# Two gated layers with a routed mixture of experts: row sums by VectorE from PSUM, their moments earlier in VectorE's order, POOL's powers behind three scatters

## The reference, cut to what matters

```
x = x + tanh(g_xattn[0]) * attention(layernorm(x), ctx, ctx)
x = x + tanh(g_ffn[0])   * ternary_ffn(layernorm(x))            # top 102 of 1024 kept per row
x = x + tanh(g_xattn[1]) * ssm(ctx, ctx, layernorm(x))          # 16 heads of 8 channels, length 256
x = x + tanh(g_ffn[1])   * moe(layernorm(x))                    # 64 experts, 6 per row, and a shared one

# ssm, per head: y = causal convolution of k_i * v_j with the head's kernel, + D * k_i * v_j
#                out_j = sum_i y_ij * q_i
# moe: softmax of x @ gate_w.T, top 6 of 64, weights normalised over the 6,
#      sum over the 6 of weight * expert(x), plus shared(x); expert = down(silu(gate) * up)
```

## Time and profile before

| | |
|---|---|
| median of three runs | 725.75 us (724.75 to 727.04) |
| the profiled execution | 725.16 us, its span 723.3 us |
| granted TensorE clock, mean | 0.929 |
| PE busy | 612.6 us, 85% |
| VectorE busy | 473.6 us, 65% |
| POOL busy | 434.3 us, 60% |
| ScalarE busy | 285.7 us, 40% |

### The profile page before, as it was taken

One profiled execution on the slowest core, in us unless ns is written; L12 is line 12 of the kernel. 1 busy time (PEld: TensorE's weight loads), 2 busy tenths in 40 slices (PEclk: granted clock), 3 DMA queues, 4 the chain that ended last, 5 costly groups with the idle time before them and its releaser, 6 DMA issues.

```text
span 723.3 us, 12095 instructions
## 1 busy us (share of the span) xinstructions
PE 612.6 (85%) x3072; PEld 472.9 (65%) x3072; DVE 473.6 (65%) x1607; ACT 285.7 (40%) x641; POOL 434.3 (60%) x483
## 2 busy tenths in 40 slices
PE   4789994873999958999998669999999999999920
PEld 2455552442988827777777458888888888888720
DVE  6898997998688768878875623454445454544425
ACT  3156777863355423444445213233323223233200
POOL 2697996130244421877777733677777777786660
PEclk9799997887999988999999669999999999999975
DMA  7457655695599955666663679999999999996878
GB/s 231 159 176 273 207 203 193 204 318 223 185 339 322 347 174 164 224 214 215 230 233 126 225 225 308 241 257 250 247 249 262 255 255 255 263 274 107 237 118 296
DMA packets 89050, 167.83 MB, mean 232 GB/s; under 512 B 11296, under 2 KB 53728, under 8 KB 88992
## 3 DMA queue, kind: packets, MB, share of 16 engines
q1 hardware_dynamic: 68096, 139.36, 57.6%
q0 software_dynamic: 20608, 27.82, 20.0%
q10 hardware_dynamic: 288, 0.01, 0.0%
HBM read 93.33 MB, written 73.81 MB: 231 GB/s over the span
## 4 chain that ended last, share of the span: by engine, by line
PE 55%; DVE 15%; issue 11%; DMA 8%; POOL 6%; ACT 3%; SPq 1%; DVEq 1%; POOLq 0%; ACTq 0%
PE psum L1123 12%; PE psum L951 8%; PE psum L1136 7%; PE psum L1127 6%; PE psum L1030 4%; PE psum L1141 4%; PE psum L1107 4%; POOL xs_rows L773 3%; DVE hh L1735 3%; PE psum L942 2%; DVE Z L1579 2%; PE psum L1041 2%; DMA acc<-hh,toki 2%; POOL acc L815 2%; PE psum L987 1%
## 5 line engine op out<-in xcount | busy, mean ns | idle before, releaser
L815 POOL DMA_INDIRECT acc<-hh,toki x128 | 187.9, 1468 | 80.5 <-DVE hh L2092 41.9
L2092 DVE TENSOR_SCALAR hh<-psum,wtok 96x256 f32<-96x256 f32 (+3 forms) x128 | 55.8, 477 | 131.8 <-issue 120.8
L773 POOL DMA_INDIRECT xs_rows<-Z,slot x96 | 98.2, 1023 | 38.5 <-issue 26.7
L1123 PE MATMUL psum<-qT,Z 128*128 128x192 f32 (+3 forms) x480 | 97.7, 347 | 0.0
L1123 PEld LDWEIGHTS psum<-qT,Z 128*128 128x128 f32 x480 | 81.0, 193 | 2.3
L690 POOL TENSOR_TENSOR rstd<-mv,neghalf 128x1 f32<-128x1 f32 (+1 forms) x48 | 33.6, 709 | 65.8 <-DVE mv L1843 57.6
L1402 ACT ACTIVATE qT<-psum 128x384 f32<-128x384 f32 (+3 forms) x64 | 33.6, 524 | 96.6 <-PE psum L1107 95.7
L872 PE MATMUL psum<-wt,hTs 128*128 128x512 f32 x128 | 59.7, 609 | 0.6 <-ACT hTs L1219 0.6
L951 PE MATMUL psum<-wt,hh 128*128 128x256 f32 x256 | 58.1, 380 | 0.0
L1136 PE MATMUL psum<-Z,hh 128*96 128x256 f32 (+3 forms) x240 | 56.7, 379 | 0.0
L1127 PE MATMUL psum<-qT,Z 128*112 128x192 f32 (+3 forms) x240 | 52.6, 342 | 0.0
(11 more groups left out here) (352 smaller groups left out, 1266.2 us busy)
## 6 DMA issues: line engine op xcount, KB each, us to landing
Z<-in_wexp SPq DMA_DIRECT2D x62, 496.0 KB, 4.1
xs_rows<-fill SPq DMA_DIRECT2D x64, 272.0 KB, 3.2
kv_rows<-Z SPq DMA_DIRECT2D x12, 688.0 KB, 3.9
kvb<-kv_rows SPq DMA_DIRECT2D x8, 688.0 KB, 6.0
Z<-co_rows SPq DMA_DIRECT2D x8, 688.0 KB
Z<-kv_rows SPq DMA_DIRECT2D x8, 688.0 KB, 6.3
Z<-xs_rows SPq DMA_DIRECT2D x24, 204.0 KB, 4.1
Z<-xs_rows SPq DMA_DIRECT2D x16, 272.0 KB, 3.8
```

Of the source, the lines that this page charges most:

```text
L773: pool.indirect_dma_start(out=xs_rows[:, :], out_offset=bass.IndirectOffsetOnAxis(ap=slot[:, t, k:k + 1], axis=0), in_=H[:, t, :], in_offs ...
L815: pool.indirect_dma_start(out=acc[a][:, :], out_offset=bass.IndirectOffsetOnAxis(ap=toki[0:p, g, j:j + 1], axis=0), in_=y_sb[0:p, s, j, :] ...
L1123: m = pe.matmul(pA[par][:, g * CAP:g * CAP + 2 * p], w[:, s, k, g * P:(g + 1) * P], xT[:, par, k, 0:2 * p], start=(k == 0), stop=(k == 1))
L2092: m = dve.tensor_scalar(y_sb[0:p, s, j, :], pY[par][0:p, j * D:(j + 1) * D], wtok[0:p, g, j:j + 1], None, ALU.mult)
```

## The change

PE's product of the rows with the identity goes, and the turned quarters start the sum in PSUM. ScalarE's `keep_rows` goes. VectorE adds the PSUM sum to the rows in place (one instruction of 128x512), ahead of the statistics, in `x3_moments`, which now holds the statistics too and signals them once for a pair. In VectorE's order `x3_moments(u)` moves ahead of `times_q(a)` for pairs from 2 on (behind it for pairs 0 and 1), `mean_shift(u)` stands behind `times_q(a)`, and `shared_hidden(w,2)` and `four(a)` behind that. POOL's power stands behind three scatters of every pair.

```
 POOL       for u in range(NPAIR):
                 pool.wait_ge(slots_ready, u + 1)
-                near = 3 if u in (0, NPAIR - 2) else K - 1
-                for k in range(near):
+                for k in range(3):
                     scatter(2 * u, k)
                 if u + 1 < NPAIR:
                     pow_pair(u + 1)
-                for k in range(near, K):
+                for k in range(3, K):
                     scatter(2 * u, k)
 PE x3_turn
-                pe.wait_ge(x_in[n // 2], 32)
-                for q in range(2):
-                    pe.matmul(x3p[:, q * D:(q + 1) * D], ident[:, :], X[:, 2 * n + q, :],
-                              start=(q == 0), stop=False, skip_group_check=True)
...
                             m = pe.matmul(x3p[:, q * D + l * P:q * D + (l + 1) * P], r[:, s_, l], ident[:, :],
-                                          start=False, stop=(s_ == 3), is_transpose=True, skip_group_check=True)
+                                          start=(q == 0 and l == 0 and s_ == 0), stop=(s_ == 3), is_transpose=True, skip_group_check=True)
 ACT
-            def keep_rows(u):
-                act.wait_ge(o3T_done, u + 1)
-                act.activation(X[:, 2 * u:2 * u + 2, :], x3p[:, :].rearrange("p (t d) -> p t d", t=2), ACT.Copy).then_inc(x3_done, 1)
 DVE
-            def x3_stats(n):
+            def x3_moments(n):
+                dve.wait_ge(x_in[n // 2], 32)
+                dve.wait_ge(o3T_done, n + 1)
+                rows = X[:, 2 * n:2 * n + 2, :]
+                dve.tensor_tensor(rows, rows, x3p[:, :].rearrange("p (t d) -> p t d", t=2), ALU.add).then_inc(x3_done, 1)
                 dve.wait_ge(x3_done, n + 1)
                 for t in range(2 * n, 2 * n + 2):
-                    alone(dve, "dve")
-                    dve.bn_stats(stats[:, t, :], X[:, t, :]).then_inc(stats_done, 1)
-
-            def x3_moments(n):
-                dve.wait_ge(stats_done, 2 * n + 2)
+                    m = dve.bn_stats(stats[:, t, :], X[:, t, :])
+                m.then_inc(stats_done, 1)
+                dve.wait_ge(stats_done, n + 1)
                 alone(dve, "dve")
...
-                if u == 1:
+                if u < 0:
                     times_q(a)
-                    x3_stats(u)
-                    shared_hidden(w, 0)
+                    four(a)
+                    times_q(b)
+                    four(b)
+                elif u < 2:
+                    times_q(a)
                     x3_moments(u)
-                    shared_hidden(w, 1)
+                    if w >= 0:
+                        shared_hidden(w, 0)
+                        shared_hidden(w, 1)
                     mean_shift(u)
                     four(a)
                     times_q(b)
-                    shared_hidden(w, 2)
+                    if w >= 0:
+                        shared_hidden(w, 2)
                     four(b)
                 else:
...
+                    shared_hidden(w, 0)
+                    shared_hidden(w, 1)
+                    x3_moments(u)
                     if heads:
                         times_q(a)
+                    mean_shift(u)
+                    shared_hidden(w, 2)
+                    if heads:
                         four(a)
...
                         times_q(b)
                         four(b)
```

More of the change, by code:

```diff
@@ L766, in _ @@
             pool.wait_ge(filled, 16 * (E + 3))
-            def pow_pair(n):
-                pool.wait_ge(var5_ready, n + 1)
-                pool.tensor_tensor(rstd[:, 2 * n:2 * n + 2], mv[:, 2 * n:2 * n + 2, 1], neghalf[:, 0:2], ALU.pow).then_inc(rstd5_ready, 1)
             def scatter(t, k):
@@ L776, in scatter, with pow_pair @@
                     in_=H[:, t, :], in_offset=None).then_inc(scattered, 16)
+            def pow_pair(n):
+                pool.wait_ge(var5_ready, n + 1)
+                pool.tensor_tensor(rstd[:, 2 * n:2 * n + 2], mv[:, 2 * n:2 * n + 2, 1], neghalf[:, 0:2], ALU.pow).then_inc(rstd5_ready, 1)
             pow_pair(0)
@@ L1380, in _ @@
                     continue
-                keep_rows(u)
                 if u >= 1:
@@ L1390, in _ @@
                 shared_silu(u, 0)
-                if u == 0:
-                    keep_rows(1)
                 shared_silu(u, 1)
@@ L1978, in _ @@
                     times_q(b)
-                    shared_hidden(w, 2)
+                    if w >= 0:
+                        shared_hidden(w, 2)
                     four(b)
                 else:
-                    if w >= 0:
-                        shared_hidden(w, 0)
-                        shared_hidden(w, 1)
+                    shared_hidden(w, 0)
+                    shared_hidden(w, 1)
+                    x3_moments(u)
                     if heads:
                         times_q(a)
+                    mean_shift(u)
+                    shared_hidden(w, 2)
+                    if heads:
                         four(a)
[L1988 to L1996, removed]
                         times_q(b)
-                    if heads:
                         four(b)
```

## The result

The changed kernel takes 734.12 us (median of 4 runs, 732.59 to 737.28); the kernel before, on the same chip, 725.44. The ratio is 1.0122, 95% interval 1.0085 to 1.016: slower by 8.7 us, where 725.3 had been forecast and 722.8 to 728.0 given as the range. The profiled execution took 734.11 us, its span 732.0.

A forecast was written before the change was run, and what follows sets the result against it. POOL's scatter stream was taken as the bound. First scatter +0.65, pair 2 0.97 later, pairs 2 to 5 at 16.5, last power -0.40, last scatter +0.1 later, the rest unchanged: 725.3 us, range 722.8 to 728.0.

The forecast's parts named there:

- rival B: Routing stage: PE was the bound, so 0.95 a pair for seven pairs is gained, 6.6 us, 718.5; chance 0.04.
- Hold (b): Steady cycle: head a's sum holds a scatter beginning 1.54 after the power, 0.05 if POOL is late, 0.8 if VectorE is.
- rival C: Routing stage: scatter holds vanish as VectorE's sums fall into issue gaps, -2.9 us, 722.3; chance 0.09.
- Hold (a): Steady cycle: POOL's power, now amid head a's products, is held 0.15, with bounds of nothing and 1.45.
- Rival D: Steady cycle: power held until head a's run of products ends, cycle 17.05, 0.45 over the present one, 727.7; chance 0.17.
- What follows the stage is unchanged.: Behind the routing stage: the change alters nothing there, so no time was added or taken.
- The start: Ahead of the first slots: VectorE's added PSUM sum, taken as 0.60, makes the first scatter come 0.65 later.
- POOL's waits for slots: Starts of pairs 2 to 6: 0.51 to 0.56 instead of 0.30, together 1.13 us; afterwards no wait but the first.

The follow-up runs named there:

- sum only: Kernel before with VectorE's sum from PSUM replacing the identity product and ScalarE's copy, old VectorE order, powers behind five: 727.7 us, 1.0036.
- order only: Changed kernel with PE's identity product and ScalarE's copy put back, new VectorE order and powers behind three kept: 729.14 us, 1.005.
- square root: Changed kernel with sums in four pieces, last turn's old order, ScalarE's root and VectorE's reciprocal replacing POOL's power, shared_hidden(w,2) right behind the moments: 728.77 us.
- late split: Changed kernel with last turn's old order, sums in four pieces except the first four heads, pair 0's rows by PE and ScalarE as before: 725.61 us.
- last: Changed kernel with shared_hidden(6,2) ahead of mean_shift(7) again in the last turn: 731.2 us, 1.0096.
- five: Changed kernel with POOL's powers behind five scatters again, three in the first pair and the last but one: 740.19 us, 1.0219.
- before, split: Kernel before with VectorE's 1024-column sums cut into four of 256 from pair 2 on: 724.76 us, 0.9999.
- three only: Kernel before with POOL's powers behind three scatters in every pair: 725.91 us, 1.0016.
- split: Changed kernel with each VectorE sum of 1024 columns cut into four of 256: 729.59 us, 1.0073.

## Why the prediction was wrong

For the cycles the bound was read rightly: POOL's stream sets the pace, work taken from PE buys nothing (sum only: slower with 0.95 less on PE), and rival B is out. What failed were the size of one hold and one thing that I did not follow. The stage is 8.84 longer than forecast: 4.66 in pairs 2 to 5 (forecast 16.5 each), 1.85 in pair 6, 2.22 behind the last scatter and 0.18 ahead of pair 2, with 0.07 less in pair 7. The last scatter, which was to be issued within 2 us of 419.4, was issued at 425.70.

**Hold (b), the sum of head a.** This is the term that was mis-sized. The prediction put the scatter that meets the sum "1.54 after the power", and so took the hold as 0.05 if POOL leads. There is an earlier scatter, 0.2 behind the power, which (b) leaves out; rival C says that a sum holds nothing if a scatter begins just ahead of it. This one begins 0.25 ahead (363.14 and 363.39) and is held to the sum's end all the same. The case stood in its own rows: the 2.04 of 292.76 is the scatter behind a power whose release also let VectorE go on to a sum, and it was read for its size only. The logic ran backwards as well: if POOL is the late one, VectorE stands waiting for the power, and then the sum falls on that scatter in each of pairs 3 to 5; in order only VectorE is the late one, by 0.1, and the scatter escapes. By terms the cycle was to be 15.9 and holds of 0.08 beside products, 0.15 at the power, 0.05 and 0.25 at the sums. The rows of pair 4 give as holds 0.26 and 0.14 beside products, 0.01 at the power, 1.34 (2.38 against the 1.04 that a scatter behind a power takes elsewhere) and 0.31: 15.9 + 2.06 = 17.96, and the cycle is 17.94. So 1.29 of the 1.5 us that the cycle is above forecast is this one term; cutting the sum took 1.0 of it back in the mean of four cycles. The short products, which the prediction said hold next to nothing, held 0.40 in this pair; the scatter of 1.51 in pair 0 before (289.03), beside such products, spoke against that reading already.

The scatter ended 0.92 behind the sum's end, so it was held for the whole of what was left of it. By the Trainium skill, "SBUF — State Buffer", section "Who interferes with whom", the second of two such instructions is blocked until the other is done; the row agrees, but which of the two is the second could not be read from the rows' starts, and in square root the block went beyond one instruction, to the end of a run of nine products (347.60 and 346.77).

**Hold (a), the power.** Forecast 0.15, measured 0 to 0.13 (0.72 to 0.85 against 0.72). Rival D had the right sign and put the cycle 0.9 too low (17.05, measured 17.94), but its mechanism is wrong for the power: the longest in any kernel here took 0.96. Scatters, not powers, were held for a run (square root, late split).

**"What follows the stage is unchanged."** This, with the last turn taken as it was, failed by 3.7 us (1.45 in pair 6, 2.2 behind the last scatter), and last showed the cause: 1.7 come back in pair 6 and 1.4 behind the last scatter. The other 0.8 there don't; in the kernels with the last turn repaired the load comes 2.3 to 3.1 behind the last scatter, and why is open. I moved shared_hidden(w,2) behind mean_shift in the cycle and priced PE's wait there at 0.6 (the row of 363.53 has 1.74), but didn't follow that edit into the last turn, where no products cover the wait for the power: PE stands 4.78, comes back at half the clock, and the slots of pair 7 come at 411.34, where the first scatter of pair 7 had begun at 405.38 before. I also had the last power not waiting, -0.40; it didn't wait, but only because POOL was 5 us late.

**The balance at the row load.** The earlier trace rows show the load released by the landing of the last scatter. I took that as the only thing that it waits for. SP's store of the shared expert's rows stands ahead of it in SP's list; before the change it ended with the landing, at 421.78, and in the kernel after it is the store that goes last (430.34).

**The start.** Forecast 0.65; the rows give 0.35 by the clock of the span, 0.76 from the last turn of the stage before. With five at 26.45 from the same instructions, the 0.76 isn't known to better than some 0.7, and 0.65 isn't refuted. The sum took 0.67 to 0.69, not 0.60. VectorE also waits 0.58 for PE's turns, which take 3.58 at a granted clock of 0.53 behind 4.60 us in which PE did nothing; before, they took 2.87 behind 3.02 (in five VectorE doesn't wait there):

```profile
270.68 3.58 PE L982 MATMUL psum<-ident,hh 128*128 128x128 f32 x16 [4.60 <-DVE hh L1886]
...
274.37 0.69 DVE L1892 TENSOR_TENSOR X<-X,psum 128x512 f32<-128x512 f32 x1 [0.58 <-PE psum L982]
```

I had left out that the identity product, which went, had stood ahead of these turns.

**POOL's waits for slots**, rows of 0.51 to 0.56, did go in pairs 3 to 6, as forecast; ahead of pair 2 one of 0.71 stayed, and the 2.12 ahead of pair 7 came new. The row of 0.50 in the kernel before with cut sums shows that the loop of slots lies right behind at some 16.4.

## What to carry to other kernels

When one event releases two engines, look at what each does next: here the power released a scatter of POOL and, by way of VectorE's wait, a long sum with two SBUF operands, and a collision that pair 0 alone had before came in every steady cycle. Follow each moved instruction into the first and the last turn, where the work that covers it in the middle is missing, and list everything that stands ahead of the last transfer on its queue. Three loops within a quarter of a microsecond of each other left little to gain here by taking work from one of them: 0.23 a cycle when POOL's hold went (before, split), nothing when PE's work did (sum only).

## What the runs showed of the hardware

- A held scatter ends 0.82 to 0.92 us behind the end of the VectorE instruction that holds it: 0.92 behind the sum where it stands right behind a power (365.52, 364.60), 0.82 behind a product (360.79, 359.97), 0.83 behind the run of products in square root (347.60, 346.77). Scatters that aren't held take 1.04 behind a power and 0.96 elsewhere, so the wait lies within the first 0.15 us, and the rest runs its full time afterwards.
- A head's products with one operand in PSUM held no scatter here: 346.72 before the change took 1.04, 365.83 after it 0.96, both beside a run of them.
- A scatter whose row begins 0.25 ahead of the sum was held (363.14), one 0.28 ahead of it was not (order only, 362.24), and one 0.03 behind it was not either (three only, 341.79). In split a scatter 0.24 ahead of the first piece wasn't held by it. The rows' starts don't order the two to better than some 0.3 us.
- Short two-operand instructions in a run hold a scatter for one of them (1.22 and 1.10 for 0.96) or to the end of the run (3.30 to 3.38 in each steady pair of square root; 1.76 in late split; 1.51 in pair 0 before). What decides is open.
- VectorE's sum of 128x512 with one operand in PSUM takes 0.67 to 0.69 us.
- Twelve products of TensorE took 2.86 us at a granted clock of 1.00, and 5.31 at 0.51 behind 4.78 us of idling.
